# Moving the LayerNorm's small steps to GpSimd and the weight transposes to earlier queue places, in an attention and feed-forward kernel on eight cores

## The reference

```python
q, k, v = x @ Wq, x @ Wk, x @ Wv
scores = where(causal_mask, -inf, q @ k.T)
attn = softmax(scores * 1024 ** -0.5)
x = layernorm(x + (attn @ v) @ Wo)
gate, up = x @ wg.T, x @ wu.T              # wg, wu [3072, 1024]
x = layernorm(x + (silu(gate) * up) @ wd.T)  # wd [1024, 3072]
```

## Time and profile before

| | us |
|---|---|
| three runs | 3403.53, 3419.33, 3455.82 |
| their median | 3419.33 |
| the profiled execution, its own time | 3395.17 |
| its span on the slowest core (core 4) | 3393.1 |
| spans of the 8 cores | 3370.0 to 3393.1 |
| busy on core 4: TensorE, VectorE, ScalarE, GpSimd | 2661.4, 603.8, 323.9, 14.8 |

### The profile page before, as it was taken

How to read it: one execution, slowest core, us unless ns; L and a number is a source line. 1 busy time by engine, 2 the same in 40 slices (tenths; PEclk the granted TensorE clock), 3 DMA queues, 4 the chain that set the end, 5 groups by cost and what they waited for, 6 DMA issues and landing times.

```text
span 3393.1 us, 35379 instructions; the slowest of 8 cores (3370.0 to 3393.1 us)
## 1 busy us (share of the span) xinstructions
PE 2661.4 (78%) x8256; PEld 805.1 (24%) x8256; DVE 603.8 (18%) x914; ACT 323.9 (10%) x629; POOL 14.8 (0%) x28
## 2 busy tenths in 40 slices
PE   0879777878863999959939787878787649999597
PEld 0223111111110333313313221111111113333243
DVE  0000111110432111103310001110114411111144
ACT  0222000010000111100002220001000001111000
POOL 0000000000000000000000000000000000000000
PEclk9989555555555999979969885555555569999799
DMA  9129950000344111042260200000004341120432
GB/s 116 39 32 118 112 62 0 0 1 0 109 118 109 32 26 37 15 81 75 88 136 1 50 1 0 0 0 0 0 16 123 109 95 26 33 43 1 85 96 93
DMA packets 254662, 176.37 MB, mean 52 GB/s; under 512 B 224976, under 2 KB 224976, under 8 KB 253648
## 3 DMA queue, kind: packets, MB, share of 16 engines
q1 hardware_dynamic: 245248, 130.07, 15.0%
q0 software_dynamic: 9232, 44.04, 10.3%
HBM read 121.63 MB, written 69.21 MB: 56 GB/s over the span
## 4 chain that ended last, share of the span: by engine, by line
PE 71%; issue 9%; DMA 8%; SPq 6%; DVE 5%; ACT 1%; DVEq 0%; POOL 0%; ACTq 0%; POOLq 0%
PE PF L555 12%; PE PF L565 12%; PE PF L465 11%; PE PF L420 11%; PE PF L365 8%; PE PF L603 6%; PE PF L502 5%; PE PF L389 4%; SPq L355 3%; PE PB L452 2%; SPq L591 2%; DMA ys_s<-ydram 2%; DMA xs<-x 2%; SPq L520 1%; DMA xbf<-x 1%
## 5 line engine op out<-in xcount | busy, mean ns | idle before, releaser
L555 PE MATMUL PF<-yT_s,wgTb_s 128*128 128x512 bf16 x1536 | 412.5, 379 | 111.6 <-DMA wgTb_s<-wgbf 111.6
L603 PE MATMUL PF<-wdT_s,h_s 128*128 128x512 bf16 x1536 | 372.1, 381 | 83.6 <-DMA wdT_s<-wdbf 80.8
L465 PE MATMUL PF<-ET_s,v_s 128*128 128x512 bf16 x640 | 364.9, 588 | 89.3 <-DVE ET_s L456 3.2
L420 PE MATMUL PF<-kT_s,qT_s 128*128 128x512 bf16 x640 | 359.5, 583 | 89.3 <-DVE sc_s L425 5.7
L565 PE MATMUL PF<-yT_s,wuTb_s 128*128 128x512 bf16 x1536 | 410.6, 376 | 0.0
L502 PE MATMUL PF<-wob_s,aoT_s 128*128 128x512 bf16 x512 | 291.2, 589 | 94.1 <-DVE r_s L507 27.1
L365 PE MATMUL PF<-xT_s,wqb_s 128*128 128x512 bf16 x512 | 135.0, 385 | 157.9 <-DMA xT_s<-xbf 157.9
L577 DVE TENSOR_TENSOR h_s<-PF,sg_s 128x512 bf16<-128x512 f32 x192 | 123.8, 686 | 747.8 <-PE PF L565 740.5
L555 PEld LDWEIGHTS PF<-yT_s,wgTb_s 128*128 128x128 bf16 x1536 | 146.7, 96 | 362.8 <-issue 274.0
L603 PEld LDWEIGHTS PF<-wdT_s,h_s 128*128 128x128 bf16 x1536 | 148.6, 97 | 306.9 <-issue 175.6
L565 PEld LDWEIGHTS PF<-yT_s,wuTb_s 128*128 128x128 bf16 x1536 | 146.7, 96 | 248.7 <-issue 161.9
(11 more groups left out here) (44 smaller groups left out, 780.3 us busy)
## 6 DMA issues: line engine op xcount, KB each, us to landing
xs<-x SPq DMA_DIRECT2D x32, 512.0 KB, 4.3
ydram<-y_s SPq DMA_DIRECT2D x32, 512.0 KB, 2.7
ys_s<-ydram SPq DMA_DIRECT2D x32, 512.0 KB, 4.1
out<-outb_s SPq DMA_DIRECT2D x32, 512.0 KB, 2.9
xbf<-x POOLq DMA_DIRECT2D x2, 4096.0 KB, 137.0
ybf<-ybb_s SPq DMA_DIRECT2D x32, 256.0 KB, 2.8
wgbf<-wg POOLq DMA_DIRECT2D x1, 6144.0 KB, 87.7
wubf<-wu POOLq DMA_DIRECT2D x1, 6144.0 KB, 144.0
```

Of the source, the lines that this page charges most:

```text
L420: e.matmul(ap, qT[:, ec, t * P:(t + 1) * P], kT[:, ec, nb * 512:(nb + 1) * 512], start=(ec == 0), stop=(ec == ND - 1)),
L465: e.matmul(ap, vtm[:, cs, vc * P:(vc + 1) * P], ET[:, cs, :], start=(cs == 0), stop=(cs == ncs - 1)),
L555: e.matmul(apg, wgTb[:, slw, dc, hl * P:(hl + 1) * P], yT[:, dc, n * 512:(n + 1) * 512], start=(dc == 0), stop=(dc == ND - 1)),
L603: e.matmul(ap, h_actT[:, hc, t * P:(t + 1) * P], wdT[:, hc, half * 512:(half + 1) * 512], start=(hc == 0), stop=(hc == NH - 1)),
```

## The change

It has five parts.

- `emit_ln` puts `negmean`, `nmean2`, `var2` and the normalising pass on GpSimd (they were on VectorE). The cast to `ybb` goes to GpSimd as well.
- `emit_wtransposes` for groups 0 and 1 is called ahead of stage 3, and for group g+2 behind the matmuls of group g.
- `wdT` is split: `wdTa` (12 transposes) is emitted ahead of the feed-forward's groups, `wdTb` (12 transposes) behind them.
- `Arena.alloc` can place a buffer at the upper end of the highest free stretch that fits, and `yT`, `wgTb`, `wuTb`, `sg`, `wdTa`, `wdTb`, `ys`, `r2` and `outb` are placed so.
- `maskt` becomes bf16, and `sqbuf` moves to another place.

```diff
-        b.op("dve", lambda e: e.tensor_scalar_mul(negmean[:, sl:sl + 1], s1[:, sl:sl + 1], -1.0 / D),
+        b.op("pool", lambda e: e.tensor_scalar_mul(negmean[:, sl:sl + 1], s1[:, sl:sl + 1], -1.0 / D),
...
-        b.op("dve", lambda e: e.tensor_scalar(dst_ap, src_ap, negmean[:, sl:sl + 1], rstd[:, sl:sl + 1],
-                                              ALU.add, ALU.mult),
+        b.op(norm_eng, lambda e: e.tensor_scalar(dst_ap, src_ap, negmean[:, sl:sl + 1], rstd[:, sl:sl + 1],
+                                                 ALU.add, ALU.mult),
...
-        yT = ar.alloc("yT" + sfx, [P, ND, S], BF16)
+        yT = ar.alloc("yT" + sfx, [P, ND, S], BF16, side="top")
+
+        wgTb = ar.alloc("wgTb" + sfx, [P, 2, ND, 512], BF16, side="top")
+        wuTb = ar.alloc("wuTb" + sfx, [P, 2, ND, 512], BF16, side="top")
+
+        def emit_wtransposes(hgrp):
+            slw = hgrp % 2
+            for dc in range(ND):
+                b.dma("sp", lambda e, dc=dc, hgrp=hgrp, slw=slw:
+                      e.dma_start_transpose(wgTb[:, slw, dc, :],
+                                            wgbf_d.ap()[hgrp * 512:(hgrp + 1) * 512, dc * P:(dc + 1) * P]),
+                      reads=[("wgbf",)], writes=[("wgTb" + sfx, slw)], key=f"wgt{slw}", coarse=True)
...
+
+        emit_wtransposes(0)
+        emit_wtransposes(1)
...
-            b.op("dve", lambda e, sl=sl: e.tensor_copy(ybb[:, sl, :], ybuf[:, sl, :]),
+            b.op("pool", lambda e, sl=sl: e.tensor_copy(ybb[:, sl, :], ybuf[:, sl, :]),
...
+        wdTa = ar.alloc("wdTa" + sfx, [P, NH // 2, D], BF16, side="top")
+        for hc in range(NH // 2):
+            b.dma("sp", lambda e, hc=hc: e.dma_start_transpose(wdTa[:, hc, :], wdbf_d.ap()[:, hc * P:(hc + 1) * P]),
...
+            if hgrp + 2 < NH // 4:
+                emit_wtransposes(hgrp + 2)
...
-        for hc in range(NH):
-            b.dma("sp", lambda e, hc=hc: e.dma_start_transpose(wdT[:, hc, :], wdbf_d.ap()[:, hc * P:(hc + 1) * P]),
+        for hc in range(NH // 2, NH):
+            b.dma("sp", lambda e, hc=hc:
+                  e.dma_start_transpose(wdTb_t[:, hc - NH // 2, :], wdbf_d.ap()[:, hc * P:(hc + 1) * P]),
```

More of the change, by code:

```diff
@@ L217, in __init__, with alloc @@
         self.peak = 0
-    def alloc(self, name, shape, dtype):
+    def alloc(self, name, shape, dtype, side="bottom"):
         nbytes = int(np.prod(shape[1:])) * mybir.dt.size(dtype)
         nbytes = (nbytes + 31) // 32 * 32
-        for ent in sorted(self.free_list, key=lambda e: e[1]):
-            if ent[1] >= nbytes:
-                off = ent[0]
+        if side == "top":
+            cands = sorted(self.free_list, key=lambda e: -e[0])
+        else:
+            cands = sorted(self.free_list, key=lambda e: e[1])
+        for ent in cands:
+            if ent[1] >= nbytes:
+                if side == "top":
+                    off = (ent[0] + ent[1] - nbytes) // 32 * 32
+                    if off < ent[0]:
+                        continue
+                    ent[1] = off - ent[0]
+                else:
+                    off = ent[0]
+                    ent[0] += nbytes
+                    ent[1] -= nbytes
                 deps = set(ent[2])
-                ent[0] += nbytes
-                ent[1] -= nbytes
                 if ent[1] == 0:
@@ L292, in build_program @@
     identb = ar.alloc("identb", [P, P], BF16)
-    maskt = ar.alloc("maskt", [P, 4, 512], F32)
+    maskt = ar.alloc("maskt", [P, 4, 512], BF16)
+    sqbuf = ar.alloc("sqbuf", [P, D], F32)
     nmax = ar.alloc("nmax", [P, 2], F32)
@@ L490, in emit_seq @@
         ybb = ar.alloc("ybb" + sfx, [P, 2, D], BF16)
-        yT = ar.alloc("yT" + sfx, [P, ND, S], BF16)
+        yT = ar.alloc("yT" + sfx, [P, ND, S], BF16, side="top")
[8 more added lines that the diff above has]
+                      reads=[("wgbf",)], writes=[("wgTb" + sfx, slw)], key=f"wgt{slw}", coarse=True)
+                b.dma("sp", lambda e, dc=dc, hgrp=hgrp, slw=slw:
+                      e.dma_start_transpose(wuTb[:, slw, dc, :],
+                                            wubf_d.ap()[hgrp * 512:(hgrp + 1) * 512, dc * P:(dc + 1) * P]),
+                      reads=[("wubf",)], writes=[("wuTb" + sfx, slw)], key=f"wut{slw}", coarse=True)
+        emit_wtransposes(0)
+        emit_wtransposes(1)
         for t in range(NT):
@@ L531, in emit_seq @@
         h_actT = ar.alloc("h" + sfx, [P, NH, S], BF16)
-        wgTb = ar.alloc("wgTb" + sfx, [P, 2, ND, 512], BF16)
-        wuTb = ar.alloc("wuTb" + sfx, [P, 2, ND, 512], BF16)
-        sg = ar.alloc("sg" + sfx, [P, 2, 512], BF16)
+        sg = ar.alloc("sg" + sfx, [P, 2, 512], BF16, side="top")
+        wdTa = ar.alloc("wdTa" + sfx, [P, NH // 2, D], BF16, side="top")
+        for hc in range(NH // 2):
+            b.dma("sp", lambda e, hc=hc: e.dma_start_transpose(wdTa[:, hc, :], wdbf_d.ap()[:, hc * P:(hc + 1) * P]),
+                  reads=[("wdbf",)], writes=[("wdTa" + sfx, hc)], key="wdta", coarse=True)
         for hgrp in range(NH // 4):
             slw = hgrp % 2
[L538 to L546, removed]
             for hl in range(4):
@@ L583, in emit_seq, with wdt_ap @@
         ar.free("sg" + sfx)
[L585 to L588, removed]
-        for hc in range(NH):
-            b.dma("sp", lambda e, hc=hc: e.dma_start_transpose(wdT[:, hc, :], wdbf_d.ap()[:, hc * P:(hc + 1) * P]),
-                  reads=[("wdbf",)], writes=[("wdT" + sfx, hc)], key="wdt", coarse=True)
+        wdTb_t = ar.alloc("wdTb" + sfx, [P, NH - NH // 2, D], BF16, side="top")
+        ys = ar.alloc("ys" + sfx, [P, 2, D], F32, side="top")
+        r2 = ar.alloc("r2" + sfx, [P, 2, D], F32, side="top")
+        outb = ar.alloc("outb" + sfx, [P, 2, D], F32, side="top")
+        for hc in range(NH // 2, NH):
+            b.dma("sp", lambda e, hc=hc:
+                  e.dma_start_transpose(wdTb_t[:, hc - NH // 2, :], wdbf_d.ap()[:, hc * P:(hc + 1) * P]),
+                  reads=[("wdbf",)], writes=[("wdTb" + sfx, hc - NH // 2)], key="wdtb", coarse=True)
+        def wdt_ap(hc, half):
+            if hc < NH // 2:
+                return wdTa[:, hc, half * 512:(half + 1) * 512], ("wdTa" + sfx, hc)
+            return wdTb_t[:, hc - NH // 2, half * 512:(half + 1) * 512], ("wdTb" + sfx, hc - NH // 2)
         for t in range(NT):
@@ L601, in emit_seq @@
                     ap, kk = pf((bz + half) * 512, 512)
-                    b.op("pe", lambda e, ap=ap, hc=hc, t=t, half=half:
-                         e.matmul(ap, h_actT[:, hc, t * P:(t + 1) * P], wdT[:, hc, half * 512:(half + 1) * 512],
+                    wap, wkey = wdt_ap(hc, half)
+                    b.op("pe", lambda e, ap=ap, hc=hc, t=t, wap=wap:
+                         e.matmul(ap, h_actT[:, hc, t * P:(t + 1) * P], wap,
                                   start=(hc == 0), stop=(hc == NH - 1)),
-                         reads=[("h" + sfx, hc, t // 4), ("wdT" + sfx, hc)], writes=list(kk))
+                         reads=[("h" + sfx, hc, t // 4), wkey], writes=list(kk))
             apz, kkz = pf(bz * 512, 1024)
```

24 lines of the change are left out of this document (12 added, 12 removed).

## The result

The changed kernel takes 3567.7 us (median of 10 runs) against 3403.7 us for the kernel before (10 runs beside it): a ratio of 1.047, 95% interval 1.0438 to 1.0501. It is 4.7% slower, 164 us by the medians, where 51 us had been forecast. The profiled execution of the changed kernel took 3616 us, with a lower granted clock on both dies (0.721 and 0.713) than the quick executions show (0.735 to 0.739), so its rows, from core 0, are used for structure, and sizes come from the medians and from the profiles of the experiments.

A forecast was written before the change was run, and what follows sets the result against it. TensorE was taken to bound most stages, load-to-load rings the output projection and sequence 1's down projection. Terms of +43.5 and +7.7 us per sequence, +51.2 on 3395.17, gave 3446.4, by the median 3471 us; range 3425 to 3540.

The forecast's parts named there:

- at nothing: Three edits priced at no cost: the bf16 mask, the transposes of groups 2 to 5, the other buffers' new places.
- The cover of groups 2 to 5: Feed-forward: 16 transposes, about 23 us, run under a group's 256 matmuls, 67 us.
- Weight transposes ahead of `xs`: Start of output projection: 32 transposes stand before tile 0's load on SyncE, first sum 39.7 us later per sequence.
- The LayerNorm on GpSimd: Slower steps add 0.9 us per output tile, 14.4 us per sequence, and 0.45 per down tile, 7.2 us in sequence 1.
- The rival of slow passes: GpSimd's normalising pass and cast take 1.6 us or more each: 3519 us, at the bound of 2.1 us 3555; chance 0.3.
- the tiny steps would not hide under the squares: LayerNorm: VectorE's two-input squares pass blocks GpSimd's small operations; without that rule 0.6 us less per tile, 29 us in all.
- The boundary: Between the sequences: the cast of x stands behind the last LayerNorm, 93.7 us instead of 51.2, cost 42.5 us once.
- Feed-forward -29.3 and down projection -24.3 us: Gains per sequence from weight transposes done ahead: 29.3 us at the feed-forward's start, 24.3 us at the down projection.
- its ring: Down projection of sequence 1: a load-to-next-load cycle sets the pace, sums 10.6 us apart, waiting for `ys`.
- the fourth rival: Down projection of sequence 1 runs at TensorE's pace of sequence 0, 12.5 us a tile: 3493 us; chance 0.1.
- The cover in sequence 0: Down projection: TensorE's 12.5 us per tile against a ring of 10.6 hides the added 0.45, gone from about 1.2 us.
- The rival in which the transposes slip ahead of attention's end: Output projection: weight transposes run during attention, so the 2 x 39.7 us fall away: 3392 us; chance 0.05.

The follow-up runs named there:

- own keys: The changed kernel with the weight transposes signalling on separate semaphores in each sequence: 3439.6 us, ratio 1.0126 to the kernel before.
- the experiment with one operand: The changed kernel with own keys, the sum of squares replaced by a maximum that reads one SBUF operand: 3420.2 us, ratio 1.0068.
- spread transposes: The changed kernel with own keys, LayerNorm and cast on VectorE, one transpose pair behind each tile's sum, `xs` and `ys` loaded two tiles ahead: 3230.4 us.

## Why the prediction was wrong

**The step that failed** is the one that put edits "at nothing": that the other buffers' new places "change no wait that I found", and that the transposes of groups 2 to 5 cost nothing under a group's matmuls. What was missed is who else waits for these transfers. The new place of `sg` in sequence 1 carries the transposes of sequence 0 as former users, the shared keys turn them into the newest transposes, and ScalarE's silu, and TensorE behind it, stood still 5 times. The transposes of `wdTa` and `wdTb` waited for one another by the same rule. Before, by the order of the kernel's allocations, `sg` lay in a stretch whose users were only `aoT`, `y` and `ybb`, in both sequences. The price by experiment is 128 us of the 164 us lost; without it the kernel is at 1.0126, 41 us over before where 51 had been forecast. The range ended at 3540, and no rival spoke of this cost. (The forecast of 3471 us stood on a median before of 3419.3 us; the median of the ten runs is 3403.7.)

The kernel's code holds what was needed. The forecast finds the stretch in which `wgTb` and `wuTb` lie and draws the wait from it, but does not do so for `sg`. In sequence 0 the new place of `sg` is harmless (its former users are `r1`, `sc`, `wob` and `ybb`); the transposes show only if the allocations are followed into sequence 1.

The cover of groups 2 to 5 was real: with own keys no wait of TensorE for a gate or up weight is left. The other edit put at nothing, the bf16 mask, shows no cost: from the end of the q and k projection to the end of attention sequence 1 takes 601.9 us before and 600.6 with own keys (core 4).

**The other steps**, by the runs:

- Weight transposes ahead of `xs`, +39.7 us: the first sum came 36.9 us later on core 0 (48.3 us after the stage's first matmul, against 11.4). The 32 issues took 43.7 us instead of 46.5. Right, a little large; 886.7 - 847.15 is also 39.55 and not 39.7.
- The LayerNorm on GpSimd, +0.9 per output tile: +0.79. The normalising pass was under-priced by 0.16 us (1.20 against 1.04), the cast was exact. The rival of slow passes fell, and with it the 1.54 us per pass that the forecast set beside it.
- That the tiny steps would not hide under the squares was the Trainium skill's rule (SBUF - State Buffer, Who interferes with whom), then without a row; the trace after (1.04 us, ending with the squares) and the experiment with one operand (0.21 us) agree with it, though the experiment does not separate the second operand from the write. Had they hidden, 0.6 us per tile would have been saved, as the forecast had it.
- The boundary, +42.5 us: 96.1 against 57.3 us with the LayerNorm alone, +39. Moving the cast's issue alone takes 34 us of it away. Right.
- Feed-forward -29.3 and down projection -24.3 us: with own keys, attention's end to feed-forward's end is +19.1 and +23.1 us on core 4 where +24.8 was forecast; the part after it is -25.3 and -21.6 us where -24.3 and -17.1 were. Right.
- The down projection of sequence 1 follows its ring only in part. The ring doesn't hold TensorE before: 137.22 us busy of 140, 633 matmuls, 0.221 us each, which makes 10.6 us per tile, and TensorE waits for VectorE 2.7 us in all. So the fourth rival's ground, that pauses make the difference between 12.5 and 10.6 us, was wrong. But the sums come behind TensorE, the last one 10.3 us after its last matmul, and they end the kernel. With the longer ring and own keys TensorE is held for 6.6 us: the stage takes 191.9 us then and 183.6 with the LayerNorm back on VectorE, +8.3 where +7.2 was forecast. The cover in sequence 0 was 12.5 - 10.6 = 1.9 us per tile, not 1.2; nothing hung on it. The window before, core 4:

```profile
3220.00:3360.00 140.00, 137.22 (x633) 61.34 (x632) 59.51 (x97) 6.72 (x27) 0.00 (x0) 1.00 0.29 95
```

- The rival in which the transposes slip ahead of attention's end fell: the first is issued at 831.04 on core 0, the stage's first matmul at 830.75.

The LayerNorm on GpSimd hurts by itself (+2.3% with its boundary), and the moved transposes with own keys help by themselves (-0.7%); both together are at +1.3%. The forecast's terms had the same signs and sizes: +79 us (2.3%) for the one and -28 us (0.8%) for the other.

## What to carry to other kernels

When buffers are moved in an arena that hands on the users of freed space, look up for every moved buffer, in every repetition of the loop, whom its writers now wait for; a wait that counts "all issued so far" on a shared semaphore becomes a wait for the newest transfer as soon as transfers are issued early. Work put ahead in an in-order queue is paid by whatever stood there: here 32 transposes ahead of one load, and a LayerNorm ahead of one cast, each cost 35 to 40 us. A ring of load, sum, normalise, store, next load is worth breaking (two loads ahead, 5% here with the spread transposes) before its links are moved between engines.

## What the runs showed of the hardware that was not expected

- TensorE's pace at the same granted clock differs by stage: in the run with spread transposes the down projection of sequence 0 makes 526 matmul records in 140 us (0.266 us each), that of sequence 1 makes 636 (0.220 us), both at 1.00 and both without pauses of note. The pauses of the ring are thus not the reason; what is stays open. The windows of core 4 in that run:

```profile
1460.00:1600.00 140.00, 138.45 (x526) 50.94 (x535) 54.80 (x93) 7.21 (x25) 0.00 (x0) 1.00 0.24 85
...
3060.00:3200.00 140.00, 139.15 (x636) 63.39 (x648) 64.40 (x105) 7.75 (x27) 0.00 (x0) 1.00 0.27 98
```

- The output projection's granted clock rose from 0.50 to 0.94 on core 4 by the loop order alone, with pauses of VectorE's making still in it (TensorE busy 47.2 of 80 us). The stages whose every matmul brings its own weights stand at 0.50: the scores and attention times v (windows 400 to 450, 500 to 560 and 700 to 760 us before, core 4), and this one in its old order. Whether the scores would rise as well was not tried.
- A 128x1 operation on GpSimd takes 0.21 us beside a VectorE pass that reads one SBUF operand and writes 128x1, and 1.04 us beside one that reads two and writes 128x1024.
